# The first half's two norms turned by DMA instead of TensorE, with a new order of work at the seam and in the opening

## The reference

```python
x = x + xattn0(ctx_1024, layernorm(x))   # latents are normalised once more inside, ctx with gamma_media/beta_media
x = x + ffn0(layernorm(x))               # 1024 hidden, plus a rank-one update made of 16 rows of each batch
x = x + xattn1(layernorm(x), ctx_1024)   # one head
x = x + experts(layernorm(x))            # 8 experts, routed by a sigmoid
```

```python
xn = layernorm(ctx) * gamma_media + beta_media
ln = layernorm(layernorm(x)) * gamma_lat + beta_lat
q = ln @ Wq + bq                         # 8 heads of 128
k, v = split(concat(xn, ln) @ Wkv + bkv) # 512 rows
out = softmax(q k^T / sqrt(128)) v @ Wo + bo
```

## Time and profile before

| | us |
|---|---|
| median of 3 runs (1826.39 to 1828.89) | 1828.03 |
| profiled execution, its time | 1824.9 |
| its span | 1823.0 |
| PE busy | 1785.5 (98%) |
| DVE busy | 1468.9 (81%) |
| ACT busy | 1328.9 (73%) |
| POOL busy | 543.6 (30%) |
| granted TensorE clock, mean | 0.998 |

### The profile page before, as it was taken

How to read it: one execution, slowest core, us unless ns; L and a number is a source line. 1 busy time by engine, 2 the same in 40 slices (tenths; PEclk the granted TensorE clock), 3 DMA queues, 4 the chain that set the end, 5 groups by cost and what they waited for, 6 DMA issues and landing times.

```text
span 1823.0 us, 40134 instructions
## 1 busy us (share of the span) xinstructions
PE 1785.5 (98%) x12818; PEld 1658.1 (91%) x12818; DVE 1468.9 (81%) x3544; ACT 1328.9 (73%) x2554; POOL 543.6 (30%) x714
## 2 busy tenths in 40 slices
PE   7999999999999999999899999999999999999999
PEld 5888888888888888888788999999999999999998
DVE  7888888888888787787567888888888888888876
ACT  5878778887778777777576677777767777776753
POOL 3354434544344533445543111111111111111100
PEclk9999999999999999999999999999999999999999
DMA  5565555545554444444619644343443434344300
GB/s 153 106 134 135 113 138 143 139 117 127 135 132 99 87 92 86 98 98 88 137 41 292 159 73 95 65 89 72 88 88 72 95 66 90 70 87 88 72 7 13
DMA packets 370652, 185.92 MB, mean 102 GB/s; under 512 B 307744, under 2 KB 355744, under 8 KB 370592
## 3 DMA queue, kind: packets, MB, share of 16 engines
q1 hardware_dynamic: 361888, 150.55, 34.5%
q0 software_dynamic: 8704, 34.61, 10.6%
HBM read 97.29 MB, written 21.23 MB: 65 GB/s over the span
## 4 chain that ended last, share of the span: by engine, by line
PE 82%; DVE 8%; issue 3%; ACT 3%; DMA 2%; POOL 1%; SPq 0%; DVEq 0%; POOLq 0%; ACTq 0%
PE ring L741 9%; PE ring L743 9%; PE ring L742 9%; PE ring L2083 8%; PE ring L2085 8%; PE ring L2084 8%; PE sim L2085 3%; PE sim L2083 3%; PE sim L2084 3%; PE sim L741 3%; PE sim L742 2%; PE sim L743 2%; PE ps_x L741 2%; PE ps_x L742 2%; PE ps_x L743 2%
## 5 line engine op out<-in xcount | busy, mean ns | idle before, releaser
L411 POOL TENSOR_SCALAR a_parts<-a_pr,a_rinv 128x512 f16<-128x512 f32 x240 | 174.5, 739 | 470.6 <-DVE a_rinv L656 411.5
L2083 PE MATMUL ring<-b_xch,b_wel 128*128 128x256 f32 x1024 | 288.6, 282 | 0.5 <-DVE b_act_e L1696 0.5
L2085 PE MATMUL ring<-b_xcl,b_weh 128*128 128x256 f32 x1024 | 286.4, 280 | 0.0
L2084 PE MATMUL ring<-b_xch,b_weh 128*128 128x256 f32 x1024 | 286.1, 279 | 0.0
L2084 PEld LDWEIGHTS ring<-b_xch,b_weh 128*128 128x128 f32 x1024 | 193.4, 189 | 0.0
L2083 PEld LDWEIGHTS ring<-b_xch,b_wel 128*128 128x128 f32 x1024 | 192.1, 188 | 0.7 <-DVE b_act_e L1696 0.7
L2085 PEld LDWEIGHTS ring<-b_xcl,b_weh 128*128 128x128 f32 x1024 | 192.1, 188 | 0.0
L504 ACT ACTIVATE a_pr<-sim,a_nmax 128x512 f32<-128x512 f32 x256 | 173.7, 688 | 21.1 <-DVE a_nmax L645 20.7
L1404 ACT ACTIVATE b_heh<-b_act_e 128x512 fp32r<-128x512 f32 x128 | 80.7, 631 | 135.8 <-DVE b_act_e L1696 114.4
L665 DVE SCALAR_TENSOR_TENSOR a_parts<-a_pr,a_rinv,a_parts 128x512 f16<-128x512 f32 x240 | 179.1, 786 | 0.0
L645 DVE TENSOR_REDUCE a_nmax<-sim 128x1 f32<-128x512 f32 x256 | 164.8, 680 | 10.1 <-PE sim L743 10.1
(11 more groups left out here) (369 smaller groups left out, 6474.3 us busy)
## 6 DMA issues: line engine op xcount, KB each, us to landing
b_w2l_raw<-in_W2T POOLq DMA_DIRECT2D x16, 1088.0 KB, 8.8
b_even_b<-rows_between SPq DMA_DIRECT2D x16, 1024.0 KB, 5.5
b_w1l_raw<-in_W1T POOLq DMA_DIRECT2D x16, 1024.0 KB, 8.4
b_w1l_raw<-in_We SPq DMA_DIRECT2D x8, 768.0 KB, 4.6
expert_halves<-b_w1h SPq DMA_DIRECT2D x8, 768.0 KB, 3.4
expert_halves<-b_w1l SPq DMA_DIRECT2D x8, 768.0 KB, 4.8
b_weh<-expert_halves SPq DMA_DIRECT2D x8, 768.0 KB, 8.7
b_wel<-expert_halves SPq DMA_DIRECT2D x8, 768.0 KB, 10.1
```

The source lines that it names most:

```text
L411: nc.gpsimd.tensor_scalar(parts[:, 0, t, :], pr[:, h % 2, t, :], rinv[:, h % 2, t:t + 1], 1.0, ALU.mult, ALU.mult).then_inc(prob_ready, 1)
L2083: nc.tensor.matmul(out, ll, rh, start=(n == 0), stop=False)
L2084: nc.tensor.matmul(out, lh, rh, start=False, stop=False)
L2085: last = nc.tensor.matmul(out, lh, rl, start=False, stop=(n == len(parts) - 1))
```

## The change

1. The two norms of batches 1 to 15 are no longer transposed on TensorE. GpSimd writes a high fp16 plane (`ln_high`) and VectorE the low plane (`ln_low`), scaled by 2^11; SyncE turns the four planes by DMA (`ln_cross`), ScalarE applies gamma/2^11 and beta to the high one (`affine_high`), and VectorE adds the low one times gamma (`joined_halves`) and makes high and low part as before. The planes have a place of their own in SBUF.
2. `ln_high` stands behind `norm_apply` at heads 0 and 2, `ln_low` at the end of heads 2 and 3, `ln_cross` behind `cross` of heads 2 and 3 on SyncE. The output projection of heads 0 to 3 waits for the residual of the batch before (`x1_ready`) instead of the affine step.
3. Opening: 10 matmuls on the identity ahead of the transposes of ctx, and 10 in place of 6 behind them.
4. Seam: GpSimd's W1 update begins at head 5 of batch 14; the zeroing of W2's padding moves from batch 0 to batch 15; the first part of W2's update comes ahead of the inverse root; W2's low part moves from head 1 to head 2. ScalarE's parts of W1 move behind O7 and V4, those of W2 to head 1 behind O0 and behind T(1,1). VectorE's row apply and first norm of the second half come behind the maxima of head 1 instead of ahead of them.

```diff
-WARM = 6
+WARM = 10
@@ sync
+        def ln_cross(b, k):
+            take(kv_ready, b * 2 - 1 + k)
+            for part in range(2):
+                take(ln_part, (b - 1) * 4 + 2 * k + part + 1)
+                sp.dma_start_transpose(ln_turned[:, k, part].rearrange("p t c q -> p (t c) q"),
+                                       ln_parts[:, k, part].rearrange("p t d -> p (t d)")).then_inc(lnT_ready, 16)
                 if nxt and h + 1 < H:
                     cross(b, h + 1)
+                if nxt and h < 3:
+                    ln_cross(b + 1, h - 1)
@@ gpsimd
+        def ln_high(b, k):
+            take(ln_ready, b * 3 + 2 * k + 1)
+            if k == 1:
+                take(ln_part, (b - 1) * 4 + 2)
+            nc.gpsimd.tensor_scalar(ln_parts[:, k, 0], (c_ln, x_ln2)[k][:], LN_SCALE, 1.0, ALU.mult, ALU.mult)\
+                .then_inc(ln_part, 1)
                     norm_apply(b + 1, h)
+                    if h != 1:
+                        ln_high(b + 1, h // 2)
@@ scalar
+        def affine_high(b, k):
+            g, bb = ((gms, bm), (gls, bl))[k]
+            act.wait_ge(lnT_ready, (b - 1) * 64 + 2 + 32 * k + 32)
+            for c in range(DC):
+                last = nc.scalar.activation(aff[:, k, c, :].rearrange("p (t q) -> p t q", t=ST), ln_turned[:, k, 0, :, c, :],
+                                            ACT.Identity, bias=bb[:, c:c + 1], scale=g[:, c:c + 1])
+            last.then_inc(aff_ready, 1)
                     if j == 1 and h == H - 4 and nxt:
-                        affine(b + 1, 0)
+                        affine_high(b + 1, 0)
                     if j == 2 and h == H - 4 and nxt:
-                        affine(b + 1, 1)
+                        affine_high(b + 1, 1)
@@ vector
+        def ln_low(b, k):
+            dve.wait_ge(ln_part, (b - 1) * 4 + 2 * k + 1)
+            nc.vector.scalar_tensor_tensor(ln_parts[:, k, 1], (c_ln, x_ln2)[k][:], LN_SCALE, ln_parts[:, k, 0],
+                                           ALU.mult, ALU.subtract).then_inc(ln_part, 1)
+        def joined_halves(b, k):
+            done = (b - 1) * 4 + 2 + 2 * k
+            dve.wait_ge(aff_ready, b * 2 + k + 1)
+            for c in range(DC):
+                last = nc.vector.scalar_tensor_tensor(
+                    aff[:, k, c, :].rearrange("p (t q) -> p t q", t=ST), ln_turned[:, k, 1, :, c, :], (gms, gls)[k][:, c:c + 1],
+                    aff[:, k, c, :].rearrange("p (t q) -> p t q", t=ST), ALU.mult, ALU.add)
+            last.then_inc(kv_hi, 1)
...
-                    kv_halves(b + 1, 0)
+                    joined_halves(b + 1, 0)
...
-                        kv_halves(b + 1, 1)
+                        joined_halves(b + 1, 1)
...
+                    if j == n - 1 and h in (2, 3) and nxt:
+                        ln_low(b + 1, h - 2)
@@ tensor
+        pe.wait_ge(pool_step, 3)
+        for _ in range(WARM):
+            nc.tensor.matmul(ring[0][:, 0:P], ident[:], ident[:], start=True, stop=True)
         transposes(0)
...
-                    if j == 0 and h == H - 4 and nxt:
-                        if prev:
-                            pe.wait_ge(x1_ready, b)
-                        transposes(b + 1)
...
-                    pe.wait_ge(aff_ready, b * 2 + 4)
+                    if prev:
+                        pe.wait_ge(x1_ready, b)
@@ second half, gpsimd ahead(h), batch 14
-            if h == 6:
+            if h == 5:
                 odd_scaled(0)
                 pool.wait_ge(split_out, 32 * E + 32)
                 update(0, "1", 0)
                 update(0, "1", 1)
+            if h == 6:
                 update(0, "1", 2)
                 update(0, "1", 3)
                 weights_added(0, "1")
@@ second half, gpsimd beside(h, done), batch 15
             if (h, done) == (0, "begin"):
+                pool.wait_ge(first.sems["kv_ready"], 2 * B)
+                for c in range(HC):
+                    nc.gpsimd.memset(f32(w2_raw[:, c * W2ROW + D:(c + 1) * W2ROW]), 0.0)
+                update(0, "2", 0)
                 rstd_of(0, "A")
-                update(0, "2", 0)
...
-            if (h, done) == (1, "probs"):
+            if (h, done) == (2, "probs"):
                 for q in range(4):
                     weight_low(0, "2", q)
@@ second half, scalar beside(h, done)
-            if (h, done) == (0, ("K", 2)):
+            if (h, done) == (0, "exps"):
+                rows_in_order(1)
+            if (h, done) == (0, ("O", 7)):
                 weight_high(0, "1", 0)
                 weight_high(0, "1", 1)
-            if (h, done) == (0, ("Q", 1)):
+            if (h, done) == (0, ("V", 4)):
                 weight_high(0, "1", 2)
                 weight_high(0, "1", 3)
             if (h, done) == (0, ("V", 5)):
                 act.wait_ge(w_ready, 4)
                 copy_high(0, "A", xth[:])
-                for q in range(4):
-                    weight_high(0, "2", q)
...
             if (h, done) == (1, ("O", 0)):
                 gelu_high(0, 1)
+                weight_high(0, "2", 0)
+                weight_high(0, "2", 1)
             if (h, done) == (1, ("T", 1, 1)):
                 gelu_high(0, 2)
+                weight_high(0, "2", 2)
+                weight_high(0, "2", 3)
@@ second half, vector
-            if h == 7:
-                rows_apply(1)
...
-            if (h, done) == (0, "begin"):
+            if (h, done) == (0, "maxima"):
+                rows_apply(1)
                 dve.sem_inc(acc_ready, 2)
                 dve.wait_ge(x1_in, 16)
                 norm_stats(0, "A", x1_s)
```

More of the change, by code:

```diff
@@ L78, in crossing, with ln_crossing @@
         return Region(low.nc, (low.top + 127) // 128 * 128 + 2 * 8 * KB + 64, 8 * KB)
+    def ln_crossing(self):
+        low = self.of["low"]
+        return Region(low.nc, (low.top + 127) // 128 * 128 + 2 * 8 * KB + 64 + 8704, 8704)
 @dataclass
@@ L221, in latent_attention @@
     crossing = mem.crossing()
+    ln_crossing = mem.ln_crossing()
+    ln_parts, ln_turned = ln_crossing.put("a_ln_parts", [P, 2, 2, ST, D], F16), ln_crossing.put(
+        "a_ln_turned", [P, 2, 2, ST, DC, P], F16)
+    gms, gls = ln_crossing.put("a_gms", [P, DC]), ln_crossing.put("a_gls", [P, DC])
     parts, turned = crossing.put("a_parts", [P, 2, ST, SK], F16), crossing.put("a_turned", [P, 2, ST, KT, P], F16)
@@ L397, in norm_apply @@
             if k != 1:
-                take(lnT_ready, b * 2 - 1 + k // 2)
+                take(lnT_ready, (b - 1) * 64 + 2)
             for t in range(ST):
@@ L474, in scalar @@
         act.wait_ge(c_small, 16 * 2)
+        nc.scalar.activation(gms[:], gm[:], ACT.Copy, scale=1.0 / LN_SCALE)
+        nc.scalar.activation(gls[:], gl[:], ACT.Copy, scale=1.0 / LN_SCALE)
         nc.scalar.activation(bq_s[:], bq_raw[:], ACT.Copy, scale=QSCALE).then_inc(bq_ready, 1)
@@ L881, in fill_count @@
         return last.at(at + last.names[at:].index(name)) + 1
-    names = ("consts", "kv_ready", "x1_ready", "x1_out", "ring_full", "ring_lo", "sim_full", "exp_done", "wo_full", "took",
+    names = ("kv_ready", "x1_ready", "x1_out", "ring_full", "ring_lo", "sim_full", "exp_done", "wo_full", "took",
              "part_hi", "part_lo", "turned")
-    sems = dict(zip(names, (consts, kv_ready, x1_ready, x1_out, ring_full, ring_lo, sim_full, exp_done, wo_full, took,
+    sems = dict(zip(names, (kv_ready, x1_ready, x1_out, ring_full, ring_lo, sim_full, exp_done, wo_full, took,
                             prob_ready, part_lo, turned_lo)))
@@ L1267, in early @@
                 for e in range(E):
-                    nc.gpsimd.memset(index[:, e:e + 1], float(e))
-                for c in range(HC):
-                    last = nc.gpsimd.memset(f32(w2_raw[:, c * W2ROW + D:(c + 1) * W2ROW]), 0.0)
+                    last = nc.gpsimd.memset(index[:, e:e + 1], float(e))
                 last.then_inc(consts, 1)
@@ L1478, in ahead, with beside @@
                 rows_in_order(0)
-            if h == 7:
+        def beside(h, done):
+            if (h, done) == (0, "exps"):
                 rows_in_order(1)
-        def beside(h, done):
-            if (h, done) == (0, ("K", 2)):
+            if (h, done) == (0, ("O", 7)):
                 weight_high(0, "1", 0)
                 weight_high(0, "1", 1)
-            if (h, done) == (0, ("Q", 1)):
+            if (h, done) == (0, ("V", 4)):
                 weight_high(0, "1", 2)
```

15 lines of the change are left out of this document (9 added, 6 removed).

## The result

The changed kernel takes 1854.82 us (median of 4, 1854.29 to 1855.73) against 1827.21 before: ratio 1.0151, 95% interval [1.0139, 1.0163]. It is slower by 28 us, where 1829.2 was forecast and the range ended at 1839. The profiled execution has a span of 1853.1.

What follows compares the result with a forecast made beforehand. TensorE, 98% busy, was taken as the bound, with ScalarE already setting the pace at O4. Turns +5.4, opening -1.1 and seam -3.1 gave +1.2 on the median 1828.03, so 1829.2 us, range 1817 to 1839.

Steps and rivals of the forecast that it cites:

- Joins at head 5: VectorE's plane additions at head 5 cost 0.8 us ahead of each half, covered by TensorE's matmuls before their use.
- Low planes at heads 2 and 3: VectorE's new low planes ahead of the maxima delay ScalarE's chain up to O4 by 0.6 us.
- the 0.79: TensorE time per turn spent on the removed transposes, 0.79 us, said to be lost waiting for ScalarE in splitting turns.
- 0.5 more in a splitting turn, and 0.15 more in a plain one: Turns that split expert weights (batches 1 to 8), or do not (9 to 13); fifteen turns together +5.4 us.
- one gap of 0.61: ScalarE's wait for Q3 in a plain turn, 0.61 us, said to absorb the low plane's 0.6.
- SyncE is no further delay: The norm's second DMA and the high plane's, 1.2 us each, fit SyncE's queue between 397.7 and 400.4.
- High planes at nothing: GpSimd's high plane for each of the two norms costs nothing, since GpSimd is busy for 30% of the span.
- Opening, -1.1: Ten warm matmuls before the first transposes raise the clock before the V matmuls: -1.1 us, bounds 0 and -1.5.
- Seam, -3.1: Batch 15 beside the second half's first batch: gain of 12 us shrinks to 6.0, low clock loses 2.9, leaving -3.1.
- The three waits: TensorE's idle times at the seam before 897.50, 901.43 and 914.79 (1.89, 1.83, 5.28 us) go except about 0.4.
- C: VectorE and GpSimd collide at heads 2 to 4, each turn grows by 1.2: +14, 1842 us; chance 0.20.
- A: The transposes' removal pays out in full, 11.9 us over the turns: -19.0 in all, 1809 us; chance 0.12.

Runs made afterwards that it cites:

- v_nojoin: Changed kernel without VectorE's four additions of the low plane in each turn (low planes still made and turned): 1843.01 us.
- v_nolow: Changed kernel without VectorE's two low planes a turn (zero planes are turned and added as before): 1842.24 us.
- v_neither: Changed kernel with neither VectorE's two low planes nor its four additions: 1826.19 us.
- q_order: Changed kernel with SyncE issuing the norms' transposing DMAs behind head 3's probabilities, both affine steps waiting for all four planes: 1877.79 us.
- v_nohigh: Changed kernel with GpSimd writing only 16 of 512 columns of each high plane: 1855.25 us.
- n_all: Changed kernel without low planes and additions, GpSimd's bias addition moved to head 6, high planes cut to 16 columns: 1825.35 us.
- o_open: Kernel before the change with only the new opening's matmuls on the identity: 1825.95 us.
- t_turns: Changed kernel with the old opening and old second half, except that W2's padding is zeroed in batch 15: 1856.12 us.
- s_seam: Kernel before the change with only the change's edits to the second half: 1832.11 us.
- f_dma: Kernel before the change with the new seam, W1's accumulating DMA held until batch 14's last low plane is made: 1825.89 us.
- v_bias: Changed kernel with GpSimd's bias addition moved from head 3 to head 6 in batches 1 to 13: 1856.54 us.
- n_bias: Changed kernel without VectorE's low planes and additions, GpSimd's bias addition moved to head 6: 1826.85 us.
- f_both: Kernel before the change with the new seam, W1's DMA behind the last transposing DMA and W2's low part at head 1: 1819.04 us.

## Why the prediction was wrong, by its steps

- **Joins at head 5: the step that failed most.** "They are covered by the 12 matmuls of O4, 24 of the output projection and 6 of scores." That counted TensorE's work and not the work that VectorE does in the same time. In the kernel before these two rows (VectorE's and PE's timeline) give the cover, which the prediction did not read:

```profile
643.97 0.69 DVE L593 TENSOR_TENSOR a_kvl<-a_aff,a_kvh 128x512 fp32r<-128x512 f32 x1
...
646.30 0.39 PE L741 MATMUL ring<-a_kvh,a_wkh 128*128 128x512 f32 x1
```

  The low part of x's half ends at 644.66 and K6 starts at 646.30, 1.6 us later. The joins need 1.75, and beside GpSimd the cast and the low part take 0.66 longer. Measured (v_nojoin): 1.0 a turn and 2.5 in the first, 15.9 of the 25.7 us of the fourteen turns; by the medians 12. The sum fits the wait: 1.75 and 0.66 less 1.64 of cover is 0.8, and K6's bracket is 0.76 to 0.87. It also says that the joins alone would be late by only 0.1 (an estimate); the rest is GpSimd's normalising, into which they push x's cast and low part. No run takes away that collision by itself. This cost stood in the text only as "without that cover each costs its 0.8", outside the bounds.
- **Low planes at heads 2 and 3: the right mechanism, mis-sized, and the 0.79 given to the wrong cause.** Forecast were stalls that eat the 0.79 and 0.5 more in a splitting turn, and 0.15 more in a plain one, where one gap of 0.61 was to absorb the lateness. v_nojoin has what this sum counted, the low planes without the joins: the fourteen turns grow by 9.8 us, where the sum gives about 5, and the mean turn by 0.75 (splitting) and 0.55 (plain). Taken out by themselves (v_nolow), the low planes are worth 0.6 in the splitting and 1.2 in the plain turn read, 0.7 and 0.9 in the mean. The 0.79 is not theirs: v_neither has no low plane and gains only 0.7 us in fourteen turns. ScalarE is late at O4 without them. As read in the trace, and not tested, the gap is used up once and the lateness arrives twice: ahead of head 3's maxima and ahead of head 4's, and through them in exps, K5's high part, Q's low part and the casts.
- **"SyncE is no further delay."** It held for x's plane only. SyncE issues ctx's low plane at 704.83 (VectorE ends it at 704.73) with the high plane of the probabilities, ready at 704.20, queued behind it. q_order shows that this wait alone decides nothing.
- **High planes at nothing:** right (v_nohigh, n_all).
- **Opening, -1.1:** not decided. The time does not move (o_open), but the interval holds -1.1 too, and the clock is up from the first V matmul on in three of twelve executions. Of the 1.7 up to the first projection, the new waits of batch 0 are some +1.3 (t_turns against s_seam), the opening some -1.3 (changed kernel against t_turns), and the rest the falls of the clock, which the profiled execution of before did not have in this form.
- **Seam, -3.1:** the forecast part is right. The three waits went, and the pause ahead of the first W2 fill is 5.68 (5.6 forecast) with a clock of 0.50 behind it; f_dma, which has only this, gives -3.65 between the two projections. What I had not seen is W1's DMA: the prediction followed GpSimd's queue, but not which other DMA is issued in that moment. It costs 4.2 and a clock of 0.54 for 3.4 us behind, and turned -3 into +3.
- **The rivals.** C had the sign, VectorE as the place and a price of 1.2 a turn. At heads 2 to 4, where it put the collisions of VectorE and GpSimd, they lengthen the pair as it said (1.85 to 2.45, back to 1.41 in v_bias), and taking this one away moves no time, because ScalarE is late as well (it also counted three new instructions there that read two SBUF tensors; there are two). At head 5, which it did not name, the same kind of collision makes 0.66 of the lateness ahead of K6, and that is untested. The Trainium skill, page "SBUF — State Buffer", section "SBUF: two separate sides", says that a VectorE instruction with two SBUF inputs and a GpSimd one exclude each other, and that the one that starts first goes through. The trace agrees: x's low part takes 1.06 where GpSimd started first and 0.69 where the two begin together, and there GpSimd takes 1.20. A could not come true: without any new work on VectorE the fourteen turns gain 0.05 to 0.7 us (n_all, n_bias, v_neither) of the 11.1.
- **Chances.** "Slower" had 0.32, and the range ended short of rival C's 1842. The range left out the case that the joins are not covered, though the text named its price: 0.8 to 1.6 in 15 batches, 12 to 24 us, would have had to widen it.

Left open: why the clock falls near 41 us in some executions and not in others with the same code up to there. The runs only show that it does, behind a pause of 1.6 to 2.2 us, in nine of the eighteen profiled executions, and that with the opening of before the first projection then stands some 1.5 us later (68.1 against 66.4 and 66.6). Left open too: what the loss at head 5 would be without the collision with GpSimd.

## What to carry to other kernels

Cover has to be read on the engine that does the added work: take the end of its last instruction ahead of the wait and the time at which the consumer asks for it, and compare the distance (1.6 us here) with the sum of all that is added in front. Counting the consumer's instructions in between is not enough. Look also at what the work behind it is pushed into: here GpSimd's normalising adds 0.66. Where an edit moves a large DMA, look for the small, urgent ones issued in the 2 us around its new place: one wait that put it behind the last transposing DMA was worth 6 us.

## What the runs showed of the hardware

- A transposing DMA (128 by 1024 fp16) lands 3.1 us after its issue in the median of every run. Issued 0.9 to 1.5 us behind the accumulating DMA of 1 MB it took 8.6 to 9.8 (seven executions), issued in the same moment 5.4 to 7.4 (three), 0.6 to 0.8 ahead of it 4.8 (five). Issued 1.3 to 1.8 ahead it took 3.1 (o_open and t_turns), yet 4.6 at 2.25 ahead in the kernel before, for which the runs show no cause.
- VectorE's two low planes (two SBUF tensors each) take 1.41 us alone and 2.45 when GpSimd's addition of 1.82 us lies in the same time; that addition takes 1.29 in the kernel before, where it starts ahead of them. A VectorE cast from SBUF with one operand is lengthened too, 0.43 to 0.72, beside GpSimd's normalising.
- After every one of the sixteen pauses of TensorE of 4.0 to 5.7 us the granted clock was 0.50 for the next 2.8 to 6.2 us. After one of 0.9 us (f_both) it stayed at 1.00. After those of 1.6 to 2.2 us near 40 us it fell in nine executions and not in nine others.
- Transposing DMAs of half the size (128 by 512 fp16) land 2.4 us after their issue and hold SyncE for 1.19 us instead of 1.23: halving them hardly shortens the queue. Four in a row take 5.4 us of it (q_order).
